# Four transformer blocks on one core: the fourth stage's scores in three split passes from its first batch, and identity turns in four of TensorE's waits

## The reference

```python
def attention(x, c, Wq, Wk, Wv, Wo, bo):          # 16 heads of 64 (block 4: of 16)
    q, k, v = x @ Wq, c @ Wk, c @ Wv
    p = softmax(einsum('bnhd,bshd->bhns', q, k) * scale)
    return einsum('bhns,bshd->bnhd', p, v) @ Wo + bo

# blocks 1 and 2
x = attention(ln(x), ln(x), ...) + x              # stages 1 and 3
x = attention(ln(x), context, ...) + x            # stages 2 and 4
a, gate = split(ln(x) @ Wp + bp)
x = (a * gelu(gate)) @ Wf + bf + x
# block 3
x = x + attention(ln(x), context, ...)            # stage 5
# block 4, with masks
x = x + attention(ln(x), ln(x), ...)              # stage 6, causal
x = x + attention(ln(x), context, ...)            # stage 7
x = x + gelu(ln(x) @ W1 + b1) @ W2 + b2
```

## Time and profile before

| | us |
|---|---|
| median of 3 runs | 1553.16 |
| lowest, highest | 1550.68, 1554.07 |
| the profiled execution's own time | 1551.07 |
| its span, first to last instruction | 1548.9 |
| TensorE busy in the span | 1499.6 (97%) |
| ScalarE, VectorE, GpSimd busy | 1011.8, 916.0, 841.8 |
| mean granted TensorE clock | 0.993 |

### The profile page before, as it was taken

The page is one execution under the profiler, slowest core; times in us unless marked ns, Lnnn a source line. Parts: engine busy times, 40 slices in busy tenths (PEclk is TensorE's granted clock), DMA queues, the critical chain, the costliest instruction groups (busy, mean ns, idle before and its releaser), DMA issues.

```text
span 1548.9 us, 37237 instructions
## 1 busy us (share of the span) xinstructions
PE 1499.6 (97%) x13750; PEld 1304.2 (84%) x13750; DVE 916.0 (59%) x2474; ACT 1011.8 (65%) x2934; POOL 841.8 (54%) x1400
## 2 busy tenths in 40 slices
PE   7999999999999999999999999999999998899998
PEld 7888888888889888878888889878888887778878
DVE  7566544455567655654554566654555568867774
ACT  6667667666661656767666672566666678678871
POOL 3665357676553544546676645346676646744431
PEclk9999999999999999999999999999999999999998
DMA  6223110001111200211000121111000121011000
GB/s 205 76 86 123 62 32 19 19 19 45 44 48 35 81 1 15 69 49 36 20 19 19 45 65 38 55 43 36 19 19 19 43 66 34 18 34 34 19 1 25
DMA packets 41617, 67.24 MB, mean 43 GB/s; under 512 B 8352, under 2 KB 16352, under 8 KB 41440
## 3 DMA queue, kind: packets, MB, share of 16 engines
q1 hardware_dynamic: 40848, 64.71, 13.1%
q10 hardware_dynamic: 592, 0.17, 0.1%
HBM read 59.33 MB, written 5.54 MB: 42 GB/s over the span
## 4 chain that ended last, share of the span: by engine, by line
PE 85%; DVE 6%; ACT 4%; issue 3%; POOL 2%; DMA 0%; SPq 0%; DVEq 0%; ACTq 0%; POOLq 0%
PE pG L1345 49%; PE pO L1345 13%; PE pG L1541 12%; PE pS L1345 10%; ACT P L1725 1%; DVE KF L1865 1%; DVE nmax L1847 1%; DVE W L1795 1%; PE pG L1598 1%; ACT QF_hi L1669 0%; DVE bn L1777 0%; DVE full L1930 0%; POOL P L1992 0%; DVE x L1910 0%; DMA whole_f<-wts 0%
## 5 line engine op out<-in xcount | busy, mean ns | idle before, releaser
L1992 POOL TENSOR_SCALAR P<-P,rinv 112x375 f32<-112x375 f32 (+1 forms) x640 | 325.8, 522 | 244.2 <-DVE rinv L1871 243.7
L1725 ACT ACTIVATE P<-pS,nmax 112x375 f32<-112x375 f32 (+1 forms) x640 | 307.9, 496 | 102.6 <-DVE nmax L1847 102.6
L1345 PE MATMUL pG<-hT_hi,W 128*128 128x224 f32 (+2 forms) x1312 | 298.1, 306 | 9.0 <-DVE W L1795 3.5
L1738 ACT ACTIVATE PT<-pG 125x336 f32<-125x336 f32 (+1 forms) x448 | 198.5, 469 | 79.4 <-PE pG L1541 78.5
L1345 PEld LDWEIGHTS pG<-hT_hi,W 128*128 128x128 f32 x1312 | 222.4, 192 | 22.7 <-issue 4.1
L1541 PE MATMUL pG<-ident,P 112*125 112x112 f32 (+1 forms) x1472 | 225.4, 278 | 8.8 <-ACT PT L1738 2.8
L1847 DVE TENSOR_REDUCE nmax<-pS 112x1 f32<-112x375 f32 (+1 forms) x448 | 227.4, 549 | 6.9 <-PE pS L1345 5.3
L1345 PE MATMUL pG<-src,W 128*128 128x376 f32 (+1 forms) x956 | 220.8, 354 | 0.3 <-ACT whole_f L1673 0.2
L1541 PEld LDWEIGHTS pG<-ident,P 112*125 112x125 f32 (+1 forms) x1472 | 185.8, 176 | 41.3 <-ACT PT L1738 5.3
L1345 PE MATMUL pG<-hT_lo,W 128*128 128x224 f32 (+2 forms) x656 | 194.9, 297 | 0.0
L1345 PEld LDWEIGHTS pG<-src,W 128*128 128x128 f32 (+1 forms) x956 | 158.9, 189 | 27.7 <-issue 25.2
(11 more groups left out here) (142 smaller groups left out, 2893.2 us busy)
## 6 DMA issues: line engine op xcount, KB each, us to landing
wraw<-wts SPq DMA_DIRECT2D x110, 256.0 KB, 2.5
src<-ctx_split SPq DMA_DIRECT2D x64, 282.0 KB, 3.1
ctx_split<-hid_lo_t SPq DMA_DIRECT2D x8, 564.0 KB, 3.6
whole_f<-wts SPq DMA_DIRECT2D x14, 256.0 KB, 5.9
V<-ctxT SPq DMA_DIRECT2D x8, 376.0 KB, 4.0
src_half<-ctx_split SPq DMA_DIRECT2D x21, 94.0 KB, 3.2
bo_b<-bo SPq DMA_DIRECT2D x10, 128.0 KB, 3.3
wraw<-wts SPq DMA_DIRECT2D x8, 64.0 KB
```

The lines of the kernel that those rows point to most:

```text
L1345: return nc.tensor.matmul(o, l, r, start=first, stop=last)
L1725: ins = act.activation(o, pS[U % 4][0:T, i * n:(i + 1) * n], ACT.Exp, bias=nmax[:, r, i:i + 1], accum_out=rsum[:, r, i:i + 1])
L1738: act.activation(o[0:sh.krows, 0:n], g[0:sh.krows, 0:n], ACT.Copy).then_inc(pt_ready, 1)
L1992: ins = pool.tensor_scalar(o, o, rinv[:, r, i:i + 1], st.nscale, ALU.mult, ALU.mult)
```

## The change

There are four edits.

1. `split` is true for the fourth stage from batch 0 on, where before it was true from batch 2 on, as in the second and fifth stages. Batches 0 and 1 of the fourth stage, eight score sets, become three fp32r passes, with the splits of 16 key tiles and 8 query tiles. For its batch 0 keys, and the queries of its first pair, `ahead` is -6 instead of -2.
2. GpSimd's costs in the planner: 1.4 in place of 1.2 for the scaling of a unit in stages 1 and 3, and 1.5 in place of 1.15 for the rounding and rest of a normed tile, in all stages.
3. A new kind of TensorE event, `warm`, turns the identity into bank 0 of `pS`: 8 times behind `trans 6 7 10`, 4 behind `trans 6 7 11`, 5 behind the last `av` and 9 behind the last `ta`. It waits for the maximum of unit 12, the last to use that bank.
4. In the opening there are 34 turns in place of 12 before the first pair, and a pair waits for the queries' weight pieces before its first half and for all before its second.

```diff
 def split(s, b):
 
-    return s in (1, 3, 4) and b > 1
+    return s == 3 or s in (1, 4) and b > 1
...
-    return order
+    return [f for e in order for f in ([e, Ev("warm", 6, B - 1, 0, WARM[e])] if e in WARM else [e])]
+
+
+WARM = {Ev("trans", 6, B - 1, 10): 8, Ev("trans", 6, B - 1, 11): 4, Ev("av", 6, B - 1, 3): 5, Ev("ta", 6, B - 1): 9}
...
-        return LATER
+        return LATER - (4. if e.s == 3 and e.b == 0 else 0.)
...
     if k == "norm":
-        return 1.2 if st.self_ else .6
-    return dict(w=2.1, tb=1.3, qm=.5, hid=1.8, lnt=1.15, k=1.65, ones=.8, rstd=.6, ctx=.9, bq=.2, xb=.7, mask=1.)[k]
+        return 1.4 if st.self_ else .6
+    return dict(w=2.1, tb=1.3, qm=.5, hid=1.8, lnt=1.5, k=1.65, ones=.8, rstd=.6, ctx=.9, bq=.2, xb=.7, mask=1.)[k]
...
+        elif e.kind == "warm":
+            needs.append(("dve", Ev("scores", 6, B - 1, H - 4)))
...
                 needed = chunks_of(e) if e.kind in PIECES else []
+                if e.kind == "qk":
+                    needed = needed[:len(needed) // 2]
                 if needed:
                     weight_split(pe, max(w_no[ch] for ch in needed) - 1)
...
-            def turn_nothing(n):
+            def turn_nothing(bank, n):
 
                 for _ in range(n):
-                    nc.tensor.transpose(pO[:, 0:128], ident[:, :], ident[:, :])
-
-            turn_nothing(18)
+                    nc.tensor.transpose(bank[:, 0:128], ident[:, :], ident[:, :])
+
+            turn_nothing(pO, 18)
...
                 if e == Ev("qk", 0, 0, 0):
-                    turn_nothing(12)
+                    turn_nothing(pO, 34)
...
                     for n, (slot, col, ks) in enumerate((st.q, st.k)[:len(e.kind)]):
                         passes = []
+                        if n:
+                            weight_split(pe, max(w_no[ch] for ch in chunks_of(e)) - 1)
...
+                elif e.kind == "warm":
+
+                    wait(pe, maxed, unit_no(6, B - 1, H - 4) + 1)
+                    turn_nothing(pS[unit_no(6, B - 1, H - 4) % 4], e.m)
```

More of the change, by code:

```diff
@@ L528, in duration @@
             return .75 if st.small else 2.83
-        return dict(ta=.48, tb=.27, q=.68, qk=1.36, k=.69 if joined(e.s, e.b) else .86, kk=.5 if e.m else .26, vp=.94, lnt=.23, ffg=1.06 if e.b else 1.4, ffa=1.06 if e.b else 1.4, ff2=2.83)[k]
+        return dict(warm=.11 * e.m, ta=.48, tb=.27, q=.68, qk=1.36, k=.69 if joined(e.s, e.b) else .86, kk=.5 if e.m else .26, vp=.94, lnt=.23, ffg=1.06 if e.b else 1.4, ffa=1.06 if e.b else 1.4, ff2=2.83)[k]
     if engine == "act":
```

## The result

The changed kernel took 1548.59 us (median of 7 runs, 1546.92 to 1549.45) and the kernel before, run beside it, 1553.10 us (7 runs, 1550.09 to 1554.07): ratio 0.9975, 95% interval 0.9965 to 0.9985. The predicted time was 1548.0. The profiled execution of the changed kernel took 1548.73 us (span 1546.7), that of the kernel before 1551.07: 2.3 us apart, of the 4.5 us between the medians. Two executions of kernels further down, at 1638.67 and 1795.86 us with mean granted clocks of 0.85, are left out of the ratios. TensorE's share of the chain is 84% instead of 85%, GpSimd's 3% instead of 2%.

The account below looks back on a forecast made before the run. The prediction took TensorE, 85% of the chain, as the bound, except in the opening, two 16-wide stages and the tail. Terms 1.2 + 0.9 + 3.15 = 5.2 us off the median 1553.16 gave 1548.0 us; 8-in-10 range 1544.0 to 1551.5.

Parts of the forecast that it names:

- Opening, 1.2 us: First projections: more turns and queries before key weights gain TensorE 2.4 us, of which 1.2 arrives (bounds 0.5 and 2.4).
- the wait of the earlier trace: Opening, at 37.80 us: TensorE's 2.04 us wait for a GpSimd scaling, fed by VectorE, was to grow longer.
- Fourth stage, 1.9 us won in eight sets: Fourth stage's first two batches: eight score sets take 1.12 us split instead of 1.36, 1.9 us gained on TensorE.
- Fourth stage, 1.0 us of stall: Fourth stage's entry: one key split slides ahead of a GpSimd scaling, delaying TensorE about 1.0 us (bounds 0 and 3.9).
- the bound of 3.9: Fourth stage's entry, rival: three key splits precede a scaling TensorE needs, 3.9 us lost, total 1550.9 us; chance 0.14.
- +0.9: Fourth stage, net: 1.9 us won in eight score sets less 1.0 us of stall, 0.9 us gained.
- the preference of -6 decides nothing on GpSimd: Fourth stage's first batch: -6 in place of -2 decides only between tasks that could start together; no size given.
- Refitted durations, 0: GpSimd's longer planned costs change only orders, showing if anywhere in the sixth and seventh stages: 0 us (bounds -1.5 and +1.5).
- Tail, 3.15 us: After the last score set: 26 turns in four waits keep the clock up at no cost, gaining 3.15 us.
- the rival of turns that don't hold it: Tail: turns at the lower clock take 0.228 us each and overrun the waits by 2.2 us, total 1553.3 us; chance 0.11.
- The 1.75 us for the output tiles: Tail's end: output tiles' 3.5 us of work at the lower clock takes 1.75 us at the full one.
- The 1.4 us ahead of them: Tail before the output tiles: ScalarE's waits for turned units vanish, bringing GpSimd's last subtraction 1.4 us earlier.

Follow-up runs that it names:

- the kernel with the turns alone: The kernel before with 34 identity turns in place of 12 in the opening and nothing else: 1549.67 us, ratio 0.9985.
- the 24 turns: The whole change plus 24 identity turns in TensorE's 3.37 us wait ahead of the third stage's last transposes: 1548.28 us, ratio 0.9971.
- the one with keys first: The kernel with turns in three more waits and the fourth stage's first batch unsplit, with the opening's queries again after the key weights: 1544.55 us, ratio 0.9948.

## Why the prediction was right, and which of its steps were not

The time (1548.6 against 1548.0) and the sign were right. The sum is right partly by luck: one term has the wrong sign in the profile and half of another rests on one execution, and differences between executions that nothing in the sum stands for make up for it.

- **Opening, 1.2 us: inside what was timed, wrong reason.** The part alone measured 1.9 us (0.5 to 3.3). TensorE did win what the steps said, 2.0 us at the first score set. But VectorE did not take it back: the wait of the earlier trace rows was to grow beyond 2.04 us and is 2.06. What took it back is the clock, which fell behind that wait (1.6 us lost between the sets at 33.80 and 44.33). So the profile keeps 0.4 us, below my lower bound of 0.5; the 1.3 us at the set at 61.67 hold the 0.9 us of the kernel before's slow VectorE operation. With no fall, as in the kernel with the turns alone, 1.6 us are kept. The order of the queries adds nothing that any timed pair shows (0.9988 against 0.9985, 0.9946 against 0.9948).
- **Fourth stage, 1.9 us won in eight sets: right.** A split set in the changed kernel goes from 705.82 to 706.94, 1.12 us, as reckoned. Over the eleven sets from the stage's first, these eight among them, the kernels with the split win 2.4 to 2.6 us. Most of the 0.5 us beyond 1.9 is a wait for ScalarE's copy of turned probabilities that I had not read: it is 0.57 or 0.58 us long in the kernel before and in two kernels without the split, and gone with it. The kernel before:

```profile
673.46 0.58 PE L1541 MATMUL pG<-ident,P 112*125 112x112 f32 x3 [0.57 <-ACT PT L1738]
```

- **Fourth stage, 1.0 us of stall: the step that failed.** I let one split slide ahead of a scaling, because I read GpSimd's free time before 630 as one gap of 0.81 us. There is a second gap, of 1.17 us, and the first split went into it:

```profile
625.93 1.78 POOL L1992 TENSOR_SCALAR P<-P,rinv 112x112 f32<-112x112 f32 x4 [1.17 <-DVE rinv L1871]
```

Two splits stand ahead of the scaling that TensorE waits for and the wait grew by 3.1 us, inside the bound of 3.9, to whose case I gave a chance of 0.14. The scaling starts 2.7 us later against the set ahead; the rest is that it took 2.24 us, where by the end of TensorE's wait it took about 1.8 before (an estimate). I had also counted no clock, which cost 1.84 us more. Lost 4.7, won 2.5: -2.2 in the profile where the sum says +0.9. Timed, the part alone is at nothing (-2.0 to +0.8 us of gain). A further quarter of a us is lost one set earlier, in every kernel with the split (the changed kernel goes from -1.14 to -0.88 us against the kernel before between the sets at 620.71 and 627.36). My reading that the preference of -6 decides nothing on GpSimd, since the planner looks at the start first, was right: written out, GpSimd's order is the same without it, and two neighbours change places on VectorE.
- **And it was not the whole of the stall.** With the splits behind the scalings the fourth stage's second set was 1.8 us late, because the reciprocal root of the normalisation stood behind the third and fourth split. Both waits removed, the part brings 2.4 us in the profile (2.2 with what is lost one set ahead) and about 2 us in time (1542.16 against 1544.23).
- **Refitted durations, 0: within its bounds, not at nothing.** Of the wait of 1.36 us at the set at 1351.69 0.23 us is left in the kernels with them, and the changed kernel wins 1.0 us between the sets at 1288.73 and 1351.69 (from +1.24 to +0.22), which the timed part (0.8 us, -0.8 to 2.2) neither confirms nor excludes.
- **Tail, 3.15 us: half of it is solid.** The clock stood at 1.00 and the turns cost 0.13 to 0.15 us each, so the rival of turns that don't hold it is refuted. The trace does not agree with the rule of the Trainium skill ("TensorE: Matmul & The Clock Gate", part 4) that the full clock does not engage for transpose mode. The 1.75 us for the output tiles measured 0.6 to 2.2 us in the second column of the table above (33.38 and 32.79 with turns, 33.96 to 34.97 without). The 1.4 us ahead of them is an artefact of my one profile: 16.7 to 17.0 us in three kernels without turns, 16.69 with them; in the profiled execution before they are 17.9 us, with low clock from 1504 on. Timed, the part is 2.5 us (1.1 to 3.9).
- **Median against profiled run.** The profiles are 2.3 us apart, the medians 4.5. I put differences read from a profile with 20.5 us of low clock ahead of its last 3 us (3.4, 3.4 and 13.7) on a median 2.1 us above it; which stretches the other executions had no profile shows. Without the slow VectorE operation the profiles would be 1.5 us apart, so 2.2 to 3.0 us stay open. The mean granted clock of every execution tells something all the same. Among 61 executions of the kernel before, beside the runs above, it is 0.991 to 0.996 (mean 0.993), and 0.001 more goes with 0.7 to 1.1 us less time; the changed kernel has 0.996 to 0.998 (mean 0.997). From these figures I estimate that roughly 3 to 4 us of the 4.5 came with the clock, which fits a gain from the turns in the opening and the tail and a split worth nothing.

## What to carry to other kernels

When work is moved to an engine with a queue of its own, list what TensorE and the other engines will next ask of that queue, and price every item placed ahead of it; here the same eight sets were worth nothing or 2 us depending on where four key splits stood. After removing one wait, read the next one: the second cost as much as most edits in this kernel. And read a wait of TensorE with the granted clock behind it: here it cost 1.6 to 1.8 us more than its length. Turns of the identity in it cost nothing that shows: the transposes behind the 24 turns start 7.2 us after the last score set ahead of them, and 7.4 us without turns.

And compare a difference between two profiles with a third kernel that leaves that stretch alone, before you give it to the change: 0.9 us here were one operation of one execution.

## What the runs showed of the chip that I had not expected

- Whether the clock falls behind a wait is not in the wait. A wait of 2.04 to 2.06 us at the same place was followed by 3.4 us at 1.2 GHz in the changed kernel, and by none in the kernel before and the one with the turns alone. All five profiled kernels with queries first and no turns there fell, none of the five with keys first and no turns there did; the times don't show the difference (0.9988 with queries first, 0.9985 without).
- A fall avoided at one place can turn up at another. Turns at 630 us removed the one at 634 and 3.4 us of low clock stood at 1300, a stretch that the profiles of five other kernels have and that of the changed kernel doesn't. With turns in three more waits besides the tail's they were gone, and not in the profile alone: the mean clock of each execution of these four kernels that enters the ratios is 0.999 or 1.000. The runs also lay closer together: 0.8 to 1.0 us apart in three of the four kernels and 2.4 us in the one with keys first, against 4.4 us for the kernel before on the same chip (1550.85 to 1555.26).
- Turns alone hold the clock, and by their own times raise it: in the opening of the changed kernel 18 took 4.10 us and the 34 soon behind them 3.88 us, 0.228 and 0.114 us each. (The granted clock reads 1.00 over both, so the rise is read from the turns.) 26 turns in four waits held 1.00 through a tail that had 0.51.
